# Relation parts written as bf16 in the prologue, and one slot in 22 blocks fetched row by row by SyncE

## The reference

```python
h_src = h_hc[src]                       # 256 features of the source node
r_uv  = r_hc[edge_type]                 # 256 features of the edge's relation
m = clifford_linear(h_src * r_uv, msg_w, msg_b)
gate = sigmoid(r_uv . gate_w + gate_b);  m = m * gate
norm = max(deg_src[src] * deg_dst[dst], 1) ** -0.5;  m = m * norm
h_agg = segment_sum(m, dst)
h_out = clifford_linear(h_hc + h_agg, upd_w, upd_b)
```

## Time and profile before

| | |
|---|---|
| time, median of 3 runs | 3798.14 us (3790.42 to 3800.16) |
| time of the profiled execution | 3788.61 us |
| its span, first to last instruction | 3786.6 us |
| PE, DVE, GpSimd busy, share of the span | 89%, 73%, 67% |

### The profile page before, as it was taken

How to read it: one execution, slowest core, us unless ns; L and a number is a source line. 1 busy time by engine, 2 the same in 40 slices (tenths; PEclk the granted TensorE clock), 3 DMA queues, 4 the chain that set the end, 5 groups by cost and what they waited for, 6 DMA issues and landing times.

```text
span 3786.6 us, 71040 instructions
## 1 busy us (share of the span) xinstructions
PE 3353.8 (89%) x23981; PEld 2695.2 (71%) x23981; DVE 2751.4 (73%) x8573; ACT 944.2 (25%) x2408; POOL 2533.2 (67%) x2525
## 2 busy tenths in 40 slices
PE   6836999999999999688999999999999999999995
PEld 6734777877777777466777777777777777777774
DVE  8988899998989998366666666666666666666655
ACT  4041344443444443201111111111111111111111
POOL 1002777777777777377777777777777777777770
PEclk9756999999999999799999999999999999999997
DMA  5342566565565655375555555555555555555552
GB/s 146 85 159 61 154 169 164 163 165 159 162 166 162 164 159 160 112 224 141 139 138 138 144 139 139 139 137 144 139 139 138 137 143 141 137 138 144 139 125 71
DMA packets 286472, 542.02 MB, mean 143 GB/s; under 512 B 78816, under 2 KB 191728, under 8 KB 286116
## 3 DMA queue, kind: packets, MB, share of 16 engines
q0 software_dynamic: 133728, 387.52, 39.2%
q1 hardware_dynamic: 132852, 132.94, 11.9%
q10 hardware_dynamic: 19536, 17.02, 1.5%
HBM read 492.60 MB, written 44.66 MB: 142 GB/s over the span
## 4 chain that ended last, share of the span: by engine, by line
PE 30%; DVE 27%; POOL 23%; issue 11%; DMA 6%; ACT 2%; DVEq 0%; SPq 0%; POOLq 0%; ACTq 0%
POOL arena L876 21%; PE psE L1001 6%; DMA arena<-t_d,srci 4%; PE psE L1041 3%; DVE relw L1869 3%; PE psE L1258 3%; PE psE L1277 3%; PE psT L986 2%; PE psY L986 2%; DVE arena L1756 2%; PE psE L1056 2%; DVE X L2001 2%; DVE arena L1844 2%; PE psY L964 2%; DVE X L2003 2%
## 5 line engine op out<-in xcount | busy, mean ns | idle before, releaser
L876 POOL DMA_INDIRECT arena<-t_d,srci x1666 | 1586.8, 952 | 561.2 <-issue 532.5
L929 POOL DMA_INDIRECT X<-t1b_d,srci x840 | 933.8, 1112 | 596.3 <-DMA t1b_d<-arena 277.3
L1001 PE MATMUL psE<-arena 128*128 128x257 f32 x3430 | 1037.7, 384 | 52.7 <-DVE arena L1909 50.8
L1909 DVE TENSOR_TENSOR arena<-arena,psT 128x257 f32<-128x257 f32 x858 | 348.7, 420 | 382.1 <-PE psT L986 209.0
L1909 DVE TENSOR_TENSOR arena<-arena,psY 128x257 f32<-128x257 f32 x857 | 348.7, 420 | 381.7 <-PE psY L986 205.8
L1001 PEld LDWEIGHTS psE<-arena 128*128 128x128 f32 x3430 | 530.2, 190 | 109.1 <-DVE arena L1909 38.0
L1041 PE MATMUL psE<-arena,X 128*128 128x256 bf16 (+1 forms) x3675 | 532.0, 275 | 0.0
L986 PE MATMUL psT<-relw,arena 126*128 126x257 bf16 x2799 | 451.9, 274 | 16.9 <-DVE arena L1900 16.9
L986 PE MATMUL psY<-relw,arena 126*128 126x257 bf16 x2793 | 449.6, 273 | 0.0
L1056 PE MATMUL psE<-X 128*128 128x256 bf16 (+1 forms) x2520 | 403.0, 274 | 37.8 <-DMA X<-t1b_d,srci 28.8
L986 PEld LDWEIGHTS psT<-relw,arena 126*128 126x128 bf16 x2799 | 271.5, 97 | 161.6 <-DVE arena L1900 17.6
(11 more groups left out here) (356 smaller groups left out, 4333.8 us busy)
## 6 DMA issues: line engine op xcount, KB each, us to landing
arena<-types_d SPq DMA_DIRECT2D x245, 220.5 KB
arena<-t_d,srci POOLq DMA_INDIRECT x1666, 3.0
X<-t1b_d,srci POOLq DMA_INDIRECT x840
arena<-acc_d SPq DMA_DIRECT2D x98, 130.0 KB
t1b_d<-arena SPq DMA_DIRECT2D x7, 1347.5 KB, 6.4
arena<-dst_p SPq DMA_DIRECT2D x400, 1.5 KB
arena<-src_p SPq DMA_DIRECT2D x400, 1.5 KB
acc_d<-arena ACTq DMA_DIRECT2D x1, 6370.0 KB, 22.5
```

The lines of the kernel that those rows point to most:

```text
L876: pool.indirect_dma_start(gath[:, n % RG, :], None, t2_d, bass.IndirectOffsetOnAxis(ap=srci[:, n:n + 1], axis=0)).then_inc(s_g[n % RG], 16)
L929: pool.indirect_dma_start(ring1[:, n % RG1, :], None, t1b_d, bass.IndirectOffsetOnAxis(ap=srci[:, at:at + 1], axis=0)).then_inc(s_g[n % RG ...
L1001: ins = nc.tensor.matmul(psE[:, b % 2, 0:DW], sel[:, n // SG % 3, k % SG, :], rows_of(n), start=False, stop=(k == C - 1))
L1909: v.tensor_tensor(rows, rows, psR[n % BANKS][:, 0:DW], ALU.mult).then_inc(s_po, 1)
```

## The change

The relations' three bf16 parts are made in the prologue, stored in DRAM as `relp_d`, and SP loads them straight into `relb` in the first pass's tail. In the second pass one slot (number 17 of its block) of blocks 5, 7, ... 47, 22 blocks in all, is left out by GpSimd; SP fetches its 128 rows with 128 DMAs of one row each, 16 after each of eight `load_types`, four blocks ahead at the earliest. The ring of gather buffers shrinks from 17 to 15, and two buffers `lone` take its place.

```diff
-RG = 17
+RG = 15
+LONE = NB // 2 - 2
+LONE_AT = 17
...
 def lone_slot(i):            # new
+    return C * (2 * i + 5) + LONE_AT
...
 def load_pair(c):            # SP, tail of the first pass
     if c == 0:
-        sp.wait_ge(s_relwd, 16)
-    else:
-        sp.wait_ge(s_split, c)
-    sp.dma_start(gw[0:q, 0:DW], relw_d[BIN * c:BIN * c + q, :]).then_inc(s_pair, 16)
+        sp.wait_ge(s_relwd, 32)
+        sp.wait_ge(s_split, 1)
+    sp.dma_start(relb[0:q, :, c, :], relp_d[BIN * c:BIN * c + q, :, :]).then_inc(s_pair, 16)
...
-    for c in {NB: (0,), NB + 1: (1, 2)}.get(b, ()):
+    for c in {NB: range(PAIRS)}.get(b, ()):
         load_pair(c)
...
-    for c in {NB + 1: (3,), NB + 2: (4, 5, 6)}.get(b, ()):
-        load_pair(c)
...
 # SP, second pass
+def lone_sources(i):
+    sp.dma_start(lone_src, lone_d[i:i + 1, :]).then_inc(s_src, 16)
+
+def lone_rows(i, j):
+    if j == 0:
+        sp.wait_ge(s_src, 16 * (i + 3))
+        if i >= 2:
+            sp.wait_ge(s_mm, summed(lone_slot(i - 2) + 1))
+    sp.load(firsts, lone_src[0:1, WINS * j:WINS * j + WINS])        # 16 registers
+    for k in range(WINS):
+        first = sp.snap(firsts[k], min_val=0, max_val=N - 1)
+        e = WINS * j + k
+        sp.dma_start(lone[e:e + 1, i % 2, :], t2_d[bass.ds(first, 1), :]).then_inc(s_lone[i % 2], 16)
...
+sp.dma_start(lone_d.rearrange("i p -> p i"),
+             srci[:, ...][:, :, C + LONE_AT], allow_slow_non_contiguous=True).then_inc(s_src, 16)
 for n in range(2, NB * SPB):
     ...
     load_types(n)
+    i, j = n // (2 * SPB) - 1, n % (2 * SPB)
+    if n == 2 * SPB - 1:
+        sp.wait_ge(s_src, 32)
+        lone_sources(0)
+    if 0 <= i < LONE and j >= 2:
+        lone_rows(i, j - 2)
+        if j == 2 * SPB - 1 and i + 1 < LONE:
+            lone_sources(i + 1)
...
 # GpSimd, gathers
-    if n % C == 0:
+    if n % C == 0 or lone_at(n) >= 0:
         continue
...
 # DVE, prologue, after the relation rows are scaled
+v.memset(rel_parts[0:q, :, :, DW:DW + 1], 0.0)
+link(v.tensor_copy(rel_parts[0:q, :, 0, 0:DW], rows))               # q = 125, 4 x 257 elements
+link(v.tensor_tensor(rest_of, rows, rel_parts[0:q, :, 0, 0:DW], ALU.subtract))
+link(v.tensor_copy(rel_parts[0:q, :, 1, 0:DW], rest_of))
+link(v.tensor_tensor(rest_of, rest_of, rel_parts[0:q, :, 1, 0:DW], ALU.subtract))
+v.tensor_copy(rel_parts[0:q, :, 2, 0:DW], rest_of).then_inc(s_relw, 1)
...
 # DVE and ACT, before the first table
+dve.wait_ge(s_relwd, 32)
+act.wait_ge(s_relwd, 32)
...
 # DVE, tail of the first pass: parts(c), seven times, becomes
+def clear_pair():
+    dve.wait_ge(s_h, WINDOWS)
+    v.memset(relb[:, :, PAIRS - 1, :], 0.0).then_inc(s_split, 1)
```

More of the change, by code:

```diff
@@ L172, in program @@
         dst_p = nc.dram_tensor("dst_p", (E + ROOMY,), I32).ap()
+        lone_d = nc.dram_tensor("lone_d", (LONE, P), I32).ap()
         types_d = nc.dram_tensor("types_d", (RANKS * RB * C, P), F16).ap()
+        relp_d = nc.dram_tensor("relp_d", (R, 3, DW + 1), BF16).ap()
         relw_d = nc.dram_tensor("relw_d", (R, DW), F32).ap()
@@ L221, in program @@
         later = t_rows[:, 0:4, :].rearrange("p r w -> p (r w)")[:, 0:-(-SLOTS // 2)].bitcast(F16)[:, 0:SLOTS]
+        rel_parts = t_rows[:, 8:14, :].rearrange("p r w -> p (r w)").bitcast(BF16)[:, 0:RK * 3 * (DW + 1)].rearrange(
+            "p (k c w) -> p k c w", c=3, w=DW + 1)
+        rel_rest = t_rows[:, 0:4, 0:DW]
         q = o - 8 * W
@@ L378, in program @@
         o += 2 * W
+        lone = work[:, o:o + 2 * W].rearrange("p (r w) -> p r w", w=W)
+        o += 2 * W
+        lone_src = work[0:1, o:o + P].bitcast(I32)
+        o += P
         f1 = work[:, o:o + 2 * H].rearrange("p (t n) -> p t n", t=2)
@@ L585, in program @@
         s_turn = sem("s_turn")
+        s_lone = [sem(f"s_lone{k}") for k in range(2)]
         s_tb = [sem(f"s_tb{h}") for h in range(2)]
@@ L597, in loads, with lone_slot, lone_at @@
             k = n % RG
-            return len([m for m in range(k, n + 1, RG) if m % C]) + (len(range(k, C * FETCHED, RG1)) if k < RG1 else 0)
+            mine = len([m for m in range(k, n + 1, RG) if m % C and lone_at(m) < 0])
+            return mine + (len(range(k, C * FETCHED, RG1)) if k < RG1 else 0)
+        def lone_slot(i):
+            return C * (2 * i + 5) + LONE_AT
+        def lone_at(n):
+            i = (n // C - 5) // 2
+            return i if 0 <= i < LONE and n == lone_slot(i) else -1
         def rows_of(n):
+            if lone_at(n) >= 0:
+                return lone[:, lone_at(n) % 2, 0:DW]
             return gath[:, n % RG, 0:DW] if n % C else own_rows[:, n // C % 2, 0:DW]
@@ L606, in landed @@
             h, i = n // C % 2, n // C // 2
+            if lone_at(n) >= 0:
+                return s_lone[lone_at(n) % 2], 16 * P * (lone_at(n) // 2 + 1)
             if n % C:
@@ L789, in _ @@
             sp.dma_start(relw_d.rearrange("(k p) d -> p k d", k=RK), rel_sb[0:RP, :, :]).then_inc(s_relwd, 16)
+            sp.dma_start(relp_d.rearrange("(k p) c w -> p k c w", k=RK), rel_parts[0:RP, :, :, :]).then_inc(s_relwd, 16)
             table()
             sp.wait_ge(s_zerod, 16)
-            sp.wait_ge(s_relwd, 16)
+            sp.wait_ge(s_relwd, 32)
             sp.wait_ge(s_td[0], 16 * 4)
@@ L818, in _ @@
             sp.wait_ge(s_idx, 1)
-            sp.wait_ge(s_split, PAIRS)
+            sp.wait_ge(s_pair, 16 * PAIRS)
             unordered(1)
@@ L832, in _ @@
             load_own(1)
+            sp.dma_start(lone_d.rearrange("i p -> p i"),
+                         srci[:, C * 4:C * 4 + LONE * 2 * C].rearrange("p (i k) -> p i k", k=2 * C)[:, :, C + LONE_AT],
+                         allow_slow_non_contiguous=True).then_inc(s_src, 16)
             for n in range(2, NB * SPB):
@@ L896, in unordered @@
                             if layer == 1:
-                                pool.wait_ge(s_relwd, 16)
+                                pool.wait_ge(s_relwd, 32)
                                 pool.indirect_dma_start(u_rel[layer][:, 0:DW], None, relw_d, bass.IndirectOffsetOnAxis(
@@ L1349, in _ @@
             pe.wait_ge(s_a, WINDOWS)
-            pe.wait_ge(s_split, PAIRS)
+            pe.wait_ge(s_pair, 16 * PAIRS)
             pe.wait_ge(s_so, NB)
@@ L1619, in second_pass @@
                 act.wait_ge(s_idx, 1)
-                act.wait_ge(s_split, PAIRS)
+                act.wait_ge(s_pair, 16 * PAIRS)
                 for k in range(XR):
@@ L1802, in _ @@
                         ins = v.tensor_copy(rel_sb[0:q, k, D:DW], glog[0:q, k:k + 1])
-                    ins.then_inc(s_relw, 1)
+                    link(ins)
+                    v.memset(rel_parts[0:q, :, :, DW:DW + 1], 0.0)
+                    rows, rest_of = rel_sb[0:q, :, :], rel_rest[0:q, :, :]
+                    link(v.tensor_copy(rel_parts[0:q, :, 0, 0:DW], rows))
[3 more added lines that the diff above has]
+                    v.tensor_copy(rel_parts[0:q, :, 2, 0:DW], rest_of).then_inc(s_relw, 1)
                     v.tensor_tensor(dstf[:, :].rearrange("p (b k) -> p b k", k=C), dsti.rearrange("p (b k) -> p b k", k=C),
@@ L2061, in first_pass @@
                             in_place(r)
-                    for c in range(PAIRS):
-                        if t == STEPS + WINS + 2 + 6 * c:
-                            parts(c)
+                    if t == STEPS + WINS + 2:
+                        clear_pair()
                     if t == STEPS + 1:
@@ L2262, in _ @@
             dve.wait_ge(s_td[1], 16 * 3)
-            dve.wait_ge(s_relwd, 16)
+            dve.wait_ge(s_relwd, 32)
             unordered(0)
```

## The result

The changed kernel takes 3804.99 us in the median of 20 runs (3797.44 to 3810.71), the kernel before 3792.30 us in 20 runs beside it (3787.25 to 3800.16): a ratio of 1.0030 [1.0023, 1.0037], or +12.7 us. The sign was right; 3940 us was far off, by the term that was to decide. SP is not the bound.

A forecast was written before the change was run, and what follows sets the result against it. GpSimd's issue was taken to bound the kernel before, SP's row fetching the changed second pass: 3788.6 + 155 - 8 (relation parts) + 2 (store, ring at the start) = 3938 us, named as 3940; range 3780 to 4040 for eight in ten.

The forecast's parts named there:

- The bound of before: Second pass: GpSimd issues gathers back to back, 85.5 us per pair of blocks; one gather fewer makes it 84.2.
- The batch of SP: Second pass: a 16-register load plus 16 one-row DMAs takes SP 10.4 us, eight per pair of blocks 83.2 us.
- the 5.7 us of other work: SP's types loads, loads of old sums and own rows, and `lone_sources`, per pair of blocks in the second pass.
- the threshold of 9.3 us per batch: Batch length from which down SP keeps up with GpSimd in the second pass: 8 x 9.3 + 5.7 + 4.2 = 84.3 us.
- the +155 us: Second pass at SP's pace: 7.6 us more per pair, 167 us over 22 pairs, less SP's 12.5 us head start.
- the idle time: Second pass: SP stands idle 4.2 us per pair of blocks, waiting for DVE's one-hots before a types load.
- the lead of 12.5 us: SP's head start in the second pass, from types loads leaving two groups before their one-hots; taken off the 167 us.
- The ring: Second pass: 15 gather buffers instead of 17 give back between 0 and 31 us of the gain, taken as 6.
- The store of `lone_d`: Second pass's start: one DMA of 2816 elements before the third types load, 0 to 10 us, taken as 2.
- The relation parts: First pass's tail saves 14 us, DVE's operations in the prologue cost 6.3 us; together -8 us.
- Rival (a): SP keeps up in the second pass and the kernel gets faster: -28 us, 3770 us as a median; chance 0.13.
- the draw: Rival: batches of 9.3 to 9.6 us, second pass within 15 us of today, 3780 to 3805 us; chance 0.08.

The follow-up runs named there:

- experiment 5: The changed kernel with `lone_src`, from which SP fills its 16 registers, 40 bytes further on in the same SBUF tile: 4021.22 us, ratio 1.0581.
- experiment 1: The kernel before with a ring of 15 gather buffers instead of 17, nothing else: 3814.86 us, ratio 1.0064.
- experiment 3: The changed kernel with 17 gather buffers again, one of the two `lone` buffers moved to `gw`: 3777.24 us, ratio 0.9961.
- experiment 7: The changed kernel, ring still 15, with SP's store of `lone_d` moved into the first pass's tail: 3787.32 us, ratio 0.9982.
- experiment 8: The changed kernel with 17 gather buffers and SP's store of `lone_d` moved into the first pass's tail: 3762.95 us, ratio 0.9917.
- experiment 4: The changed kernel with 17 gather buffers and the store of `lone_d` issued by ACT instead of SP: 3759.83 us, ratio 0.9924.

## Why the prediction was wrong, step by step

**The bound of before: right.** GpSimd's issue sets the pace; with the ring kept, a pair with one gather fewer takes 84.3 to 84.5 us for the 84.2 worked out.

**The batch of SP: the step that failed.** The form of the sum was right: the row's 0.43 us (0.42 measured), the 5.7 us of other work, and the threshold of 9.3 us per batch. The term that was mis-sized is its first, "one load of 16 registers is 3.46 us": it took 1.23. A batch of 8.0 us instead of 10.4 lies on the other side of the threshold, so the +155 us were never due. The price came from the only load of that length in the trace, and the prediction took it for the price of the operation when it was the price of that load where its data stood. With the load put at such a place (experiment 5) the batch is 10.3 us and a pair 95.4 (10.4 and 93.1 in the prediction; the idle time was 5.8 us for 4.2, and the lead of 12.5 us does not show), and the profiled span 216 us longer than the changed kernel's: the forecast's mechanism exists, this change just isn't in it.

The Trainium skill ("DMA: Bandwidth & Descriptors", Latency and other measured facts) has about 600 ns as the floor of such a load, and the prediction set it aside because no row went under 3.27 us. The loads here went down to 1.13 us: above the page's floor, but far under the bound that 25 rows of one line had seemed to give. The trace of before held a hint as well, the load of 7 registers ahead of the first edges (by source line, columns as in the earlier trace rows):

```profile
L684 SPq TENSOR_LOAD <-start_i x7: 930/1472/5836, 47.1 to 140.9; - x7
```

One length with several prices says that something besides the length counts, and 7 registers for 0.93 us make 3.46 for 16 look dear.

**The ring: mis-sized.** 6 us were taken between 0 and 31. It is 27 us alone (22 x 1.23, experiment 1; 21 of it in stops) and 24 in the changed kernel (22 x 1.10, experiment 3 against it), nearly the upper end. "No wait for PE exceeds 0.3 us" was read as slack; it says only that 17 buffers were enough, not that fewer are.

**The store of `lone_d`: mis-sized.** 2 us were taken between 0 and 10; the first pair lost 19 us. Experiment 7 shows that the store's place is the cause. What was left out is that SP's next issue stands still behind it, so that the types loads came late by their issue, not by their landing alone. This and the ring overlap: with the ring of 17 the store costs the first pair 19.2 us (94.2 against 75.0, experiment 8), with 15 it costs 16.0 (93.5 against 77.5, experiment 7).

**The relation parts: right.** In the tail, from DVE's features of block 46 (line 2090, now 2140) to the first gather, 72.0 us became 57.5: -14.5 for -14, and no wait for `gw` is left. The prologue cost less than the 6.3 us worked out. DVE's timeline there:

```profile
203.49 0.68 DVE L1858 CAST arena<-arena 125x1028 bf16<-125x1028 f32 x1
203.54 0.07 DVE L1856 MEMSET arena<- 125x12 bf16 x1
204.20 1.23 DVE L1859 TENSOR_TENSOR arena<-arena 125x1028 f32<-125x1028 f32 x1
205.47 0.70 DVE L1860 CAST arena<-arena 125x1028 bf16<-125x1028 f32 x1
206.20 1.23 DVE L1861 TENSOR_TENSOR arena<-arena 125x1028 f32<-125x1028 f32 x1
207.47 0.70 DVE L1862 CAST arena<-arena 125x1028 bf16<-125x1028 f32 x1
208.08 1.94 DVE L1863 TENSOR_TENSOR dstf<-dstf,b 128x1715 f32<-128x1715 int32 x1
```

The operation of the earlier trace rows starts at 208.08 instead of 203.37: 4.7 us. The subtractions took 1.23 us, near the 1.16 scaled from the earlier trace rows, but a cast only 0.70. Of the 9.8 us that tail and prologue give, 5.5 arrive at the first gather in this profile (8 were forecast); the first pass in between was some 4 us longer. That is no single case: from the first pass's first gather to DVE's features of block 46 the two profiles of kernels without the new parts took 1234.8 and 1235.2 us, the eight with them 1237.3 to 1244.7. So 2 to 10 us of the gain were lost there each time, a term that the prediction does not have; its cause is open.

**The rivals.** Rival (a) had the mechanism, with a chance of 0.13. Its price of -28 us needs the ring and the store at 6 and 2; at their measured 24 and 19 the same sum is -27.6 + 24 - 8 + 19 = +7, against 13.4 between the two profiled spans; of the 6 that are left 3 are the first sum's (5 us earlier instead of 8), and the rest is in the second pair and in the skipped gathers, which gave 26.4 (22 x 1.20, experiment 3 against before). So the sign of the forecast came out right for another reason than the one that it gave, which is luck. The range (3780 to 4040) held the time only because it reached down to the draw, which wasn't the draw described either: no batch was near 9.3 us.

## What to carry to other kernels

A price from one line of a trace is the price of that line: where a change rests on it, look for the same operation elsewhere in the trace, and if its price varies there, keep both ends in the forecast with weight. When buffers are taken from a ring whose producer never waits, that says nothing of what one fewer costs; here two of 17 cost 21 to 27 us, about as much as the skipped gathers gave. And a single awkward DMA is paid by whatever is queued behind it: put it where its queue is idle.

## What the runs showed of the hardware

- A load of 16 registers from one partition of SBUF took 1.13 to 1.40 us (176 loads) with the words beginning at a multiple of 64 bytes from the tile's start, and 3.43 to 3.70 us (176 loads) 40 bytes further on. Only that one shift was run; whether 16, 32 or 64 bytes is what counts is open.
- A DMA of one row is issued in 0.23 us, and 0.42 us from row to row with its register work and the move: 2816 of them stood on SP's queue, and with the ring of 17 the pairs took 84.3 to 84.5 us, as GpSimd's 67 gathers need (84.2).
- A store of 2816 single elements of 4 bytes took 0.45 us to issue itself on SP, but a later issue on that queue then took 9.5 us (11.8 in experiment 3); on ACT's queue its own issue took 7.6 us (8.1 in experiment 4). In SP's idle stretch it cost no time that the runs show.
